# A graph network kernel: where three stages read their operands, and where one bias is added

## The reference, cut to what matters

```python
h = jnp.maximum(_layernorm(x, axis=-1), 0.0)
edge_input = jnp.concatenate([h[row], h[col], edge_attr, d_raw], axis=-1)
t = jax.nn.silu(edge_input @ ew1 + eb1)
m_ij = jax.nn.silu(t @ ew2 + eb2)
agg = jax.ops.segment_sum(m_ij, row, num_segments=n)
upd = jax.nn.silu(jnp.concatenate([h, agg], -1) @ nw1 + nb1) @ nw2 + nb2
x = x + h + upd
# two layers of this, 4 heads of 32 channels, then 1 head of 64
e = alpha_src[src] + alpha_dst[dst]
e = jnp.where(e > 0, e, NEG_SLOPE * e)
alpha = _segment_softmax(e, dst, n)
out = jax.ops.segment_sum(h[src] * alpha[:, :, None], dst, num_segments=n)
```

## Time and profile before

| | |
|---|---|
| Median of three runs (lowest, highest) | 9172.81 us (9167.3, 9173.32) |
| The profiled execution | 9175.25 us, its span 9173.7 us |
| Busy in the span | TensorE 77%, VectorE 66%, ScalarE 53%, GpSimd 69% |
| Mean granted clock of TensorE | 0.703 of 2.4 GHz |
| DMA | 491.42 MB, mean 54 GB/s |

### The profile page before, as it was taken

How to read it: one execution, slowest core, us unless ns; L and a number is a source line. 1 busy time by engine, 2 the same in 40 slices (tenths; PEclk the granted TensorE clock), 3 DMA queues, 4 the chain that set the end, 5 groups by cost and what they waited for, 6 DMA issues and landing times.

```text
span 9173.7 us, 232222 instructions
## 1 busy us (share of the span) xinstructions
PE 7037.3 (77%) x51014; PEld 5502.8 (60%) x51015; DVE 6077.1 (66%) x27239; ACT 4887.5 (53%) x11854; POOL 6338.1 (69%) x7563
## 2 busy tenths in 40 slices
PE   2466666666679999995999999999957777777776
PEld 2355555555568888883566666666635555555554
DVE  7777742222234444444999999999967776676766
ACT  4122233333335455552676767767637777777775
POOL 0377777777777777771777777777737777777775
PEclk9988888888889999996555555555555555555555
DMA  4222222222222222221222222222341111111114
GB/s 141 46 55 55 55 59 60 59 60 60 59 77 80 81 81 80 80 79 25 55 55 54 55 54 54 54 54 55 53 27 28 28 28 28 28 28 28 28 28 27
DMA packets 990523, 491.42 MB, mean 54 GB/s; under 512 B 830665, under 2 KB 841468, under 8 KB 990140
## 3 DMA queue, kind: packets, MB, share of 16 engines
q0 software_dynamic: 168832, 302.29, 15.1%
q1 hardware_dynamic: 701756, 169.41, 10.0%
q10 hardware_dynamic: 119840, 18.68, 1.2%
HBM read 356.46 MB, written 151.48 MB: 55 GB/s over the span
## 4 chain that ended last, share of the span: by engine, by line
PE 24%; issue 24%; POOL 24%; DVE 17%; DMA 6%; DVEq 2%; ACT 1%; POOLq 1%; SPq 0%; ACTq 0%
POOL z_s L640 18%; POOL arena L690 6%; DMA arena<-table,arena 5%; PE ps_all L965 5%; PE ps_all L975 4%; PE ps_all L1100 3%; PE ps_all L992 3%; PE ps_all L989 2%; DVE shift L1531 2%; DVE arena L1535 2%; DVE arena L1490 2%; PE ps_all L1076 1%; DVE arena L1576 1%; PE ps_all L1001 1%; PE ps_all L977 1%
## 5 line engine op out<-in xcount | busy, mean ns | idle before, releaser
L690 POOL DMA_INDIRECT arena<-table,arena x3616 | 3479.3, 962 | 1497.8 <-issue 983.5
L640 POOL DMA_INDIRECT z_s<-arena x1660 | 1758.1, 1059 | 852.4 <-issue 504.2
L1100 PE MATMUL ps_all<-arena 128*128 128x132 f32 (+1 forms) x7232 | 1805.1, 428 | 1.8 <-DVE acc L1593 1.8
L1100 PEld LDWEIGHTS ps_all<-arena 128*128 128x128 f32 x7232 | 1603.0, 324 | 2.6 <-issue 2.6
L829 ACT ACTIVATE arena<-lanes_b,arena 128x128 bf16<-128x128 bf16 x3616 | 1147.3, 387 | 416.7 <-DVE arena L1464 388.5
L1490 DVE TENSOR_REDUCE arena<-ps_all 128x2 f32<-128x1024 f32 x904 | 1096.8, 1213 | 18.3 <-PE ps_all L1117 18.3
L1117 PE MATMUL ps_all<-arena,pick 28*128 28x512 bf16 (+1 forms) x2260 | 1072.1, 591 | 1.8 <-DVE arena L1490 1.8
L1076 PE MATMUL ps_all<-ident_b,arena 128*128 128x128 bf16 x3616 | 537.6, 301 | 651.1 <-DMA arena<-table,arena 445.9
L745 ACT ACTIVATE arena<-ps_all 18x512 f32<-18x512 f32 x415 | 243.6, 587 | 1379.9 <-PE ps_all L952 1376.4
L853 ACT ACTIVATE arena<-ps_all 28x512 bf16<-28x512 bf16 (+1 forms) x904 | 523.4, 579 | 720.1 <-PE ps_all L1076 720.1
L1386 DVE TENSOR_TENSOR arena<-lanes,arena 128x512 f32<-128x512 f32 x452 | 325.4, 720 | 758.4 <-PE ps_all L965 758.4
(11 more groups left out here) (260 smaller groups left out, 16049.3 us busy)
## 6 DMA issues: line engine op xcount, KB each, us to landing
arena<-z_s SPq DMA_DIRECT2D x452, 264.0 KB, 2.7
arena<-table,arena POOLq DMA_INDIRECT x3616
arena<-rec_d SPq DMA_DIRECT2D x1660, 10.0 KB
z_s<-arena POOLq DMA_INDIRECT x1660
rec_d<-in_rec ACTq DMA_DIRECT2D x1, 16160.0 KB, 58.2
arena<-ids_d SPq DMA_DIRECT2D x904, 4.0 KB
arena<-pos_d ACTq DMA_DIRECT2D x830, 0.5 KB
arena<-pos_d SPq DMA_DIRECT2D x830, 0.5 KB
```

What stands on the lines that cost most here:

```text
L640: pool.indirect_dma_start(z_s, bass.IndirectOffsetOnAxis(ap=slot[:, g.slot(SLOTS), u:u + 1], axis=0), z_out[:, g.slot(SLOTS), u, :], None) ...
L690: pool.indirect_dma_start(g_rows[:, r, u * step + CODE_WORDS:(u + 1) * step], None, tables[n], bass.IndirectOffsetOnAxis(ap=ids[:, r, 0, u ...
L1100: mm = pe.matmul(ps[6][:, 0:out_w], a_hot_f[:, g.slot(4), u, :], g_msg[:, g.slot(4), u * out_w:(u + 1) * out_w], start=(u == 0), stop=(u = ...
```

## The change

Three parts. In bring, the count, the zero and `lanes` that VectorE reads are kept in PSUM banks 6 and 7; ranking's running sum of parts 1 to 3 is written there too. In the edge MLP the matmul of the bias goes; VectorE adds the bias from PSUM into `msg`, and ScalarE's Silu works on `msg` in place; `msg` gets four buffers and `hot_f` eight, and the last stages move by one. In attention `picks` and the codes beside them have 128 rows in place of 28 and 19; the rows beyond are zero in `picks`, and `turned` is cleared once ahead of the first layer.

```diff
-        picks = [sb(f"pick{n}", [CODE + 3 * h, h, P], BF16) for n, (h, _) in enumerate(LAYERS)]
+        picks = [sb(f"pick{n}", [P, h, P], BF16) for n, (h, _) in enumerate(LAYERS)]
-        ones_b = sb("ones_b", [P, P], BF16)
-        b_mid = sb("b_mid", [1, F_HID])
-        b_rest = sb("b_rest", [1, F_HID])
-        b_part = sb("b_part", [1, 3, F_HID], BF16)
-        b_rows = sb("b_rows", [P, F_HID], BF16)
+        b_mid = sb("b_mid", [P, F_HID])
-        hot_f, at = carve(at, [4, U, P])
+        hot_f, at = carve(at, [SLOTS, U, P])
-        msg, at = carve(at, [2, U, F_HID])
+        msg, at = carve(at, [4, U, F_HID])
+        counted_ps, zero_ps, lanes_ps = ps[6], ps[7][:, P:P + 1], ps[7][:, 0:P]
...
@@ SP: b_mid is loaded to all partitions; b_rows is not
-            sp.wait_ge(S("b_part_ready"), 1)
-            sp.dma_start(b_rows[0:3, :], b_part.rearrange("a k f -> a (k f)")).then_inc(S("rows_in"), 16)
+            sp.wait_ge(S("w_dist_ready"), 1)
             sp.dma_start(w_edge[KX - 2:KX - 1, :], w_dist).then_inc(S("rows_in"), 16)
@@ ScalarE, edge_mlp
                 g = of(3)
-                    act.wait_ge(S("hidden2"), g.done())
-                    if g.back(2).exists():
-                        act.wait_ge(S("summed"), g.back(2).done())
-                    act.activation(msg[:, g.slot(2)].rearrange("p u f -> p (u f)"), ps[4 + g.slot(2)], ACT.Silu
-                                   ).then_inc(S("message_ready"), 1)
+                    act.wait_ge(S("biased"), g.done())
+                    act.activation(msg[:, g.slot(4)], msg[:, g.slot(4)], ACT.Silu).then_inc(S("message_ready"), 1)
@@ TensorE, edge_mlp
-                g = of(4)
+                g = of(5)
-                        mm = pe.matmul(ps[6 + r][:, 0:F_HID], hot_f[:, g.slot(4), u, :], msg[:, r, u, :],
+                        mm = pe.matmul(ps[6 + r][:, 0:F_HID], hot_f[:, g.slot(SLOTS), u, :], msg[:, g.slot(4), u, :],
                 g = of(3)
-                        pe.wait_ge(S("message_ready"), g.back(2).done())
+                        pe.wait_ge(S("biased"), g.back(2).done())
                     for u in range(U):
-                        pe.matmul(ps[4 + r][:, u * P:(u + 1) * P], mid_e[:, r, u * P:(u + 1) * P], w_mid,
-                                  start=(u == 0), stop=False, skip_group_check=True)
-                    mm = pe.matmul(ps[4 + r].rearrange("p (u f) -> p u f", u=U), ones_b,
-                                   b_rows.unsqueeze(1).broadcast_to([P, U, F_HID]), start=False, stop=True,
-                                   skip_group_check=True)
+                        mm = pe.matmul(ps[4 + r][:, u * P:(u + 1) * P], mid_e[:, r, u * P:(u + 1) * P], w_mid, start=True, stop=True)
-            edge_pipeline(pe, GROUPS, 4, edge_mlp)
+            edge_pipeline(pe, GROUPS, 5, edge_mlp)
@@ TensorE, attention
-                            mm = pe.matmul(bank, picks[n][:, h, :], turned[0:CODE + 3 * heads, g.slot(SLOTS), 1, :], start=True, stop=True)
+                            mm = pe.matmul(bank, picks[n][:, h, :], turned[:, g.slot(SLOTS), 1, :], start=True, stop=True)
@@ VectorE, rank
-                found, counted = src_hit[:, 0:PARTS[k]], src_scan[:, 0:PARTS[k]]
+                found = src_hit[:, 0:PARTS[k]]
+                counted, nought = (src_scan[:, 0:PARTS[k]], zero) if k == 0 else (counted_ps[:, 0:PARTS[k]], zero_ps)
-                dve.tensor_tensor_scan(counted, found, zero.broadcast_to([P, PARTS[k]]), come, ALU.add, ALU.add).then_inc(small, 1)
+                dve.tensor_tensor_scan(counted, found, nought.broadcast_to([P, PARTS[k]]), come, ALU.add, ALU.add).then_inc(small, 1)
-                dve.tensor_scalar(come, src_scan[:, PARTS[k] - 1:PARTS[k]], 1.0, None, ALU.mult).then_inc(small, 1)
+                dve.tensor_scalar(come, counted[:, PARTS[k] - 1:PARTS[k]], 1.0, None, ALU.mult).then_inc(small, 1)
@@ VectorE, before bring: five instructions on b_part go
+            link(dve.memset(zero_ps, 0.0))
+            link(dve.tensor_copy(lanes_ps, lanes))
@@ VectorE, bring
-                dve.tensor_tensor(dst_hot[:, r], lanes.unsqueeze(1).broadcast_to([P, U, P]),
+                dve.tensor_tensor(dst_hot[:, r], lanes_ps.unsqueeze(1).broadcast_to([P, U, P]),
@@ VectorE, edge_mlp: first in the step, ahead of the sums, hot and hot_f
+                g = of(3)
+                if g is not None:
+                    dve.wait_ge(S("hidden2"), g.done())
+                    if g.back(4).exists():
+                        dve.wait_ge(S("summed"), g.back(4).done())
+                    dve.tensor_tensor(msg[:, g.slot(4)], ps[4 + g.slot(2)].rearrange("p (u f) -> p u f", u=U),
+                                      b_mid.unsqueeze(1).broadcast_to([P, U, F_HID]), ALU.add).then_inc(S("biased"), 1)
-                g = of(5)
+                g = of(6)
...
-                    if g.back(4).exists():
-                        dve.wait_ge(S("summed"), g.back(4).done())
+                    if g.back(SLOTS).exists():
+                        dve.wait_ge(S("summed"), g.back(SLOTS).done())
@@ VectorE, attention
+                if n == 0:
+                    link(dve.memset(turned[:, :, 1, :], 0.0))
                 dve.sem_inc(S("table_ready"), 1)
```

More of the change, by code:

```diff
@@ L407, in _ @@
                     sp.dma_start(to[:, part_cols(k)], edges_of(ends, k).rearrange("(p j) -> p j", p=P)).then_inc(S(name), 16)
-            sp.wait_ge(S("weights_clear"), 2)
+            sp.wait_ge(S("weights_clear"), 1)
             loads = [
@@ L413, in _ @@
                 (w_edge[KX - 1:KX, :], eb1.rearrange("(a n) -> a n", a=1)),
-                (w_mid, ew2), (b_mid, eb2.rearrange("(a n) -> a n", a=1)),
+                (w_mid, ew2), (b_mid, eb2.rearrange("(a n) -> a n", a=1).broadcast_to([P, F_HID])),
                 (w_node_h, nw1[0:F_IN, :]), (w_node_a, nw1[F_IN:, :]), (w_out, nw2),
@@ L532, in _ @@
             pool.memset(w_edge, 0.0).then_inc(S("weights_clear"), 1)
-            pool.memset(b_rows, 0.0).then_inc(S("weights_clear"), 1)
             pool.memset(ident, 0.0).then_inc(S("const0"), 1)
@@ L921, in _ @@
                       ).then_inc(S("tables_shown"), 1)
-            pe.wait_ge(S("rows_in"), 32)
+            pe.wait_ge(S("rows_in"), 16)
             pe.wait_ge(S("chunks_ready"), 1)
@@ L1151, in _ @@
             link(dve.tensor_scalar(lane_rest, lane_col, -1.0, float(P), ALU.mult, ALU.add))
-            link(dve.memset(ones_b, 1.0))
             link(dve.memset(lane_code, 0.0))
@@ L1297, in _ @@
             link(dve.tensor_scalar(w_dist, w_dist, 1.0 / CUTOFF, None, ALU.mult))
-            link(dve.tensor_copy(b_part[:, 0, :], b_mid))
-            link(dve.tensor_tensor(b_rest, b_mid, b_part[:, 0, :], ALU.subtract))
-            link(dve.tensor_copy(b_part[:, 1, :], b_rest))
-            link(dve.tensor_tensor(b_rest, b_rest, b_part[:, 1, :], ALU.subtract))
-            link(dve.tensor_copy(b_part[:, 2, :], b_rest))
-            dve.sem_inc(S("b_part_ready"), 1)
+            dve.sem_inc(S("w_dist_ready"), 1)
+            link(dve.memset(zero_ps, 0.0))
+            link(dve.tensor_copy(lanes_ps, lanes))
             dve.wait_ge(S("ordered"), 1)
@@ L1383, in edge_mlp @@
                                       ).then_inc(S("hot_ready"), 1)
-                    if g.back(4).exists():
-                        dve.wait_ge(S("summed"), g.back(4).done())
-                    dve.tensor_tensor(hot_f[:, g.slot(4)], lanes.unsqueeze(1).broadcast_to([P, U, P]), lane, ALU.is_equal
+                    if g.back(SLOTS).exists():
+                        dve.wait_ge(S("summed"), g.back(SLOTS).done())
+                    dve.tensor_tensor(hot_f[:, g.slot(SLOTS)], lanes.unsqueeze(1).broadcast_to([P, U, P]), lane, ALU.is_equal
                                       ).then_inc(S("hot_ready"), 1)
             src_buckets = Rounds(dve, mybir.EngineType.DVE, src_bucket, NT - 1, SLOTS, 2 * SLOTS)
-            edge_pipeline(dve, GROUPS, 5, edge_mlp, src_buckets.load)
+            edge_pipeline(dve, GROUPS, 6, edge_mlp, src_buckets.load)
             dve.wait_ge(S("added"), GROUPS)
```

## The result

The kernel after takes 9078.31 us (median of four runs, 9075.95 to 9082.84), the kernel before 9173.06 in the same comparison: 0.990 of it, 95% interval 0.9888 to 0.9911. That is 95 us off where the prediction had 255.5, and outside its range of 8895 to 8995. The span fell by 99.6 us, from 9173.7 to 9074.1.

The account below looks back on a forecast made before the run. Bounds differ by stage: GpSimd in bring and layer 1, TensorE in edge MLP, VectorE in layer 0. 161 + 97 + 2 - 3.5 - 1 = 255.5 us off 9175.25 gave 8920; range 8895 to 8995.

Parts of the forecast that it names:

- layer 0's zero: Attention, layer 0: no change in time, since VectorE is busy 2118.86 of 2200 us and does not wait for TensorE.
- The part on picks and clock: Attention: 128-row picks cost zero; the grant may rise from 0.55 but gains zero, at most 18 us; the memset costs 3.5.
- Bring: Bring stage: PSUM operands stop VectorE blocking GpSimd's scatters; 161 us off, bounds 166 and 120, 5.06 us a ranking super.
- two clauses: Bring, skill's SBUF page: two-input VectorE instructions contend with GpSimd, gain stands; or tensor_tensor does not stall its DMA, gain nothing.
- Rival D: Bring: VectorE sets the pace of ranking because PSUM costs it time; up to 51 us lost, 8971 us; chance 0.07.
- bound for this cost: Bring, VectorE's PSUM operands: taken as zero, at most 0.35 us a super, 51 us in all.
- Rival C: Bring: scatters are not freed, as VectorE as such or its tensor_scalar holds them; 9081 us; chance 0.06.
- Edge MLP: Edge MLP: removing the bias matmul from always-busy TensorE saves 0.215 us a group, 97 us, bounds 70 and 99.
- Rival B: Edge MLP: GpSimd's own products set the pace, between 3.145 and 3.36 us a group; 8970 to 9017 us; chance 0.12.
- Rival E: Attention, layer 0: the higher TensorE clock gains 95 us, giving 8825 us; chance 0.04.
- rival F: Bring: PSUM streams at half rate where VectorE reads and writes it, making the kernel slower than before; chance 0.02.
- Setup: Before the first records: five b_part instructions go, two come, one DMA less is issued; 2 us off.

Follow-up runs that it names:

- e5: Kernel before with the attention part alone (128-row picks, zero fill) and 127 added VectorE instructions to keep the loop's place: 9173.1 us, 1.0012 of before.
- e1: Kernel after with 88 harmless wait instructions added at the head of VectorE's program: 8915.0 us, 0.9725 of before.
- e3: Kernel before with 40 wait instructions added, so its layer 0 loop stands where the kernel after's does: 9330.73 us, 1.0179 of before.
- e2: Kernel after with 128 wait instructions added at the head of VectorE's program: 9078.96 us, 0.9904 of before.
- e8: Kernel before with only dst_hot's lanes read from PSUM, ranking as it was, and 126 added instructions: 9113.75 us, 0.9946 of before.
- e7: Kernel before with only the ranking's count and zero in PSUM, lanes still read from SBUF, and 126 added instructions: 9079.28 us, 0.9909 of before.
- e6: Kernel before with the edge MLP part alone and 91 added instructions for the same place of the loop: 9073.77 us, 0.9904 of before.
- e4: Kernel after with the attention part undone (picks of 28 and 19 rows, no zero fill): 9073.54 us, 0.9897 of before.

## Why the prediction was wrong

**The step that failed** is layer 0's zero: "layer 0 and 1 as long as now, whatever the clock". The part on picks and clock was right: 128 rows cost nothing and the clock pays nothing (e5). What the zero left out is that the other parts of the change, the edge MLP's above all, put VectorE's loop of layer 0 40 instructions further down its program, and that it is then fetched anew at each turn: 157.2 us in layer 0. With the loop in a good place the change is worth 253 us (e1: 9168.19 to 8915.0), and 255.5 were forecast; in the new place it loses 157 of them, as does the kernel before when it is moved by 40 with nothing else changed (e3). The sum had every term of the work and none for the code.

That transfers of instructions come with the stops is seen in the traces; why they are needed from some places only is argued from the numbers. 8.2 KB a transfer and a pattern of 128 places fit stretches of 128 instructions, if one takes 64 bytes. A loop of 356 touches three of them from 384 - 356 + 1 = 29 of 128 places, and four from the others. If four stretches fit in store and one is wanted ahead, three stay and four push each other out. The 4.9 transfers a turn would be those four and the next. The lists don't say where in them a stretch begins, so the count couldn't tell beforehand which places are good.

Runs e1 to e3 show this behaviour; a page's rule bears on it. The Trainium skill ("Runtime: NRT & Kernel Launch", section "Instruction fetch mechanics") says that most engines hold 32 KiB of instructions, 512, in two blocks of 16 KiB, and that a taken branch to a block that isn't there waits for its fetch. The stop at the turn agrees. The block does not: with two blocks of 256, 157 places in a row out of 256 would be good, but 99 is good while 11 and 139 (e2 stands 128 behind the kernel after) are long, which leaves room for 127 at most. The measurement decides: transfers of 8.2 KB and a period of 128.

**Layer 1 and the fetches.** The loop of layer 1 moved by 40 too and is fetched anew too (the kernel after has 247 transfers from 6900 to 8900 us, the kernel before 3), but that stage lost nothing: GpSimd paces it, 1660 gathers in 2100 us against 1663. A stop of 2.4 us costs its length only on the engine that sets the pace.

**Bring** was right in mechanism and size. No scatter takes longer than 1173 ns, where the longest took 1591. A super while ranking takes 600/475 x 4 = 5.05 us, forecast 5.06. e8 changes nothing but where one of two operands is read, and frees 67 us: the second operand in SBUF is what holds the scatters beside `dst_hot`. In e7, the ranking's half, results go to PSUM as well, so reads and writes were not parted there. The prediction quoted two clauses that spoke against each other; these runs go with the first. Rival D (VectorE paces ranking) did not come: it is busy 537.46 of 600 us. That VectorE writes PSUM costs nothing, as taken. Groups by line of the kernel after, 500 to 1100 us (busy, mean | idle before):

```profile
L1229 DVE TENSOR_TENSOR_SCAN ps_all<-acc,carry,ps_all 128x434 f32<-128x434 f32 x120 | 135.0, 1125 | 14.5
...
L1329 DVE CAST arena<-arena 128x4 f32<-128x4 int32 x119 | 21.1, 178 | 29.1 <-DMA z_s<-arena 27.2
```

The scan takes 1125 ns; it took 1.12 us from and to SBUF. The masked multiply behind it (line 1243 before, 1233 after) takes 675 ns on the mean where it took 671. (The prediction's bound for this cost is slightly off in its own terms: five times 0.12 less 0.27 is 0.33 us a super, 49 in all, not 0.35 and 51. Nothing hangs on it.) The wait for scatters of eight supers ago fell from 102.3 us to 27.2.

**Rival C** was priced at 9081, 3 us from what was measured, and it is false: the scatters are freed. Whoever had only the total would have taken it for the truth. The stages tell them apart at once.

**Edge MLP**: 93.8 us for 97 forecast, within the bounds of 70 to 99. TensorE is still busy without a gap at the full clock, and the chain from 2550 to 3800 us has lost line 977 and nothing has come in its place:

```profile
by line: PE ps_all L959 30.0%; PE ps_all L969 28.5%; PE ps_all L982 20.6%; PE ps_all L979 13.9%; PE ps_all L991 7.1%
```

Rival B (GpSimd's products set the pace) did not come; e6 alone gave the same. The bias on VectorE takes 692 ns, 0.69 forecast.

**Rival E** (the clock pays) is out by e5, **rival F** (PSUM at half rate) by the scan. Setup: the first scatter came 2.7 us earlier, 2 were forecast.

## What to carry to other kernels

An edit that adds or takes away instructions ahead of a long loop moves the loop. Here that alone was worth 157 us, nearly as much as the bring part (165) and more than the edge MLP part (94). Before pricing an edit, count the loop's instructions and look at the page's row of the instruction queue; after it, compare that row first, and when it has jumped, shift the loop by some dozens of harmless instructions in an idle stretch and measure again. Keep a ledger by stage: here the total agreed with a rival that was false.

## What was not expected of the hardware

- A loop of 356 VectorE instructions: some 65 instruction transfers in the whole kernel from two of the places tried (85 and 99), some 595 from four others (10, 11, 35, 115), with about 2.9 us a turn on top at place 11 (157/54).
- A loop of five instructions turns in 2.34 or 2.56 us by its place (e5 and e2 against e7 and e8, one instruction apart), with no more instruction transfers: 4 from 45 to 180 us in each of the four. Of the numbers tried only 192 is slow. What decides there is open.
- The granted clock in layer 0, a mean over stretches at 1.2 and at 2.4 GHz, rose from 0.55 to 0.81 by feeding the picking matmul 128 rows instead of 28, at the same columns and less busy time (e5), and fell back with them (e4). In layer 1, from 19 rows to 128, it stayed at 0.50. Why it rose in one only is open.
